# Single float32 products in place of three float32r products, gated sums shared by three engines, and the scores of two units ahead of both value sums

## What is computed

```python
xn = _layernorm(x)
Q = (xn @ Wq.T).reshape(H, b, s, dkh); K = ...; V = ...      # the reshape mixes heads, batches and tokens
scores = einsum('hbqd,hbkd->hbqk', Q, K)
out = einsum('hbqk,hbkd->hbqd', softmax(scores), V).reshape(b, s, -1)
y = out + xn
attention = (y - mean(y, (1, 2))) / sqrt(var(y, (1, 2)) + EPS)
logits = xn @ w_gate.T
top_logits, top_idx = top_k(logits, 2); gates = softmax(top_logits) spread over the 8 experts
ffn = sum over e of gates[:, e] * ((xn @ w_in[e].T) @ w_out[e].T)
return x + attention + ffn
```

## Time and profile before

| what | value |
|---|---|
| median of 3 runs | 1052.1 us (1048.34 to 1052.39) |
| the profiled execution, its own time | 1055.4 us |
| its span, first to last instruction | 1053.6 us |
| PE busy | 1012.4 us (96%) |
| DVE busy | 873.8 us (83%) |
| ACT busy | 627.3 us (60%) |
| POOL busy | 78.7 us (7%) |
| mean granted TensorE clock | 0.981 |
| chain of work that ended last | PE 89%, DVE 5%, DMA 4% |

### The profile page before, as it was taken

One profiled execution on the slowest core, in us unless ns is written; L12 is line 12 of the kernel. 1 busy time (PEld: TensorE's weight loads), 2 busy tenths in 40 slices (PEclk: granted clock), 3 DMA queues, 4 the chain that ended last, 5 costly groups with the idle time before them and its releaser, 6 DMA issues.

```text
span 1053.6 us, 20712 instructions
## 1 busy us (share of the span) xinstructions
PE 1012.4 (96%) x7816; PEld 527.1 (50%) x7816; DVE 873.8 (83%) x1255; ACT 627.3 (60%) x1231; POOL 78.7 (7%) x205
## 2 busy tenths in 40 slices
PE   6778999999999999999999999999999999999995
PEld 6666888888886533333333333333333333333332
DVE  4301777877877989999999999999999999999976
ACT  2100111111110178888888888888888888888885
POOL 2100111011100001000100010001000100010001
PEclk9899999999999989999999999999999999999998
DMA  7777456445555012222222222222222222222214
GB/s 274 271 246 223 130 161 181 129 133 158 144 162 160 5 52 62 71 61 70 62 70 62 69 61 69 62 70 61 70 62 71 60 70 61 71 60 71 63 25 160
DMA packets 127042, 108.58 MB, mean 103 GB/s; under 512 B 81120, under 2 KB 102368, under 8 KB 126944
## 3 DMA queue, kind: packets, MB, share of 16 engines
q1 hardware_dynamic: 114016, 86.03, 29.6%
q10 hardware_dynamic: 12928, 21.24, 5.9%
HBM read 80.75 MB, written 42.21 MB: 117 GB/s over the span
## 4 chain that ended last, share of the span: by engine, by line
PE 89%; DVE 5%; DMA 4%; issue 1%; SPq 0%; ACT 0%; ACTq 0%; POOL 0%; POOLq 0%; DVEq 0%
PE ps L892 27%; PE ps L874 22%; PE ps L829 15%; PE ps L862 11%; PE ps L801 5%; PE ps L775 3%; DMA wp<-w_out_t 3%; PE ps L790 2%; PE ps L903 2%; DVE negm L620 1%; PE ps L915 1%; DVE acc L608 1%; PE ps L763 1%; DVE xnc L733 0%; DMA qf<-ot 0%
## 5 line engine op out<-in xcount | busy, mean ns | idle before, releaser
L620 DVE TENSOR_REDUCE negm<-ps 128x1 f32<-128x1024 f32 x512 | 618.5, 1222 | 31.9 <-PE ps L862 15.3
L464 ACT ACTIVATE wp<-ps 128x512 f32<-128x512 f32 x684 | 369.4, 602 | 88.7 <-PE ps L874 62.6
L874 PE MATMUL ps<-qf,kf 50*128 50x512 f32 x1024 | 388.1, 455 | 2.1 <-DVE ps L679 1.7
L862 PE MATMUL ps<-kf,qf 48*128 48x512 f32 x1024 | 368.1, 451 | 0.2 <-DVE negm L620 0.2
L874 PEld LDWEIGHTS ps<-qf,kf 50*128 50x128 f32 x1024 | 160.5, 186 | 207.4 <-ACT wp L464 107.7
L892 PE MATMUL ps<-wp,vb 128*17 128x256 f32 x2736 | 215.7, 387 | 0.3 <-issue 0.3
L862 PEld LDWEIGHTS ps<-kf,qf 48*128 48x128 f32 x1024 | 146.3, 186 | 7.5 <-issue 5.7
L464 ACT ACTIVATE vstage<-ps 128x512 f32<-128x512 f32 x170 | 102.3, 602 | 24.6 <-PE ps L874 11.2
L829 PE MATMUL ps<-mth,xth 128*128 128x512 f32 x256 | 103.8, 405 | 3.4 <-DVE spare L552 2.4
L892 PEld LDWEIGHTS ps<-wp,vb 128*17 128x17 f32 x2736 | 46.9, 95 | 118.5 <-ACT picks L464 42.8
L464 ACT ACTIVATE picks<-ps 128x512 f32<-128x512 f32 x170 | 102.4, 602 | 0.0
(11 more groups left out here) (104 smaller groups left out, 675.9 us busy)
## 6 DMA issues: line engine op xcount, KB each, us to landing
feat_d<-qk_d SPq DMA_DIRECT2D x64, 256.0 KB, 4.5
qf<-feat_d SPq DMA_DIRECT2D x128, 128.0 KB
wp<-w_in SPq DMA_DIRECT2D x16, 512.0 KB, 4.3
wp<-w_out_t SPq DMA_DIRECT2D x16, 512.0 KB, 5.2
qk_d<-stage ACTq DMA_DIRECT2D x32, 256.0 KB
qk_d<-spare ACTq DMA_DIRECT2D x32, 256.0 KB
qf<-feat_d SPq DMA_DIRECT2D x128, 64.0 KB
kf<-feat_d SPq DMA_DIRECT2D x128, 64.0 KB
```

Source lines behind the costliest of these rows:

```text
L464: nc.scalar.activation(weight_tile(n, j, b)[:, h * HALF:(h + 1) * HALF], ps[:, ST_BANK[(2 * unit + b) % 3], :], ACT.Exp).then_inc(exp_done, 1)
L620: nc.vector.tensor_reduce(negm[:, n % 2, qt:qt + 1], ps[:, b:b + 2, :].rearrange("p b c -> p (b c)"), AX.X, ALU.max, negate=True).then_inc ...
L862: last = nc.tensor.matmul(ps[:, MAX_BANK[turn % 2] + half, :], qf[rows, u, qt * P:(qt + 1) * P], kf[rows, u, :], start=True, stop=True)
L874: nc.tensor.matmul(ps[:, ST_BANK[(2 * unit + half) % 3], :], kf[rows, u, j * P:(j + 1) * P], qf[rows, u, h * HALF:(h + 1) * HALF], start=T ...
```

## The change

- All operands are plain float32; the split halves, their buffers and the instructions that make them are gone (on ACT, DVE and POOL). Each product of three is one float32 product (`project_qk`, `project_v`, `y_bank`).
- In the attention a product has 16 or 17 rows, and the four products of a unit lie on four row groups of 32 rows: the maxima on groups 0 and 1, the scores on groups 2 and 3.
- The gated sums: DVE takes two of the four banks of a tile, ACT scales the other two (`scale_experts`), and POOL adds the pieces (`add_scaled`).
- Six pairs of buffers for expert weights instead of two, and two chunks of tokens projected in the first stage instead of one.
- The stores of Q, K and V are issued by SP instead of ACT; the stored size is halved. A block is regrouped once inside the attention loop, 8 blocks ahead.
- On PE two units' `crossed_scores` stand first (h = 0 and 1), then both `sum_values`.

```diff
-    TERMS = 3
-    FR = DH * TERMS
-    SR = FR + 2
-    ROWS = P // 2
+    GROUP = 32
+    GROUPS = P // GROUP
+    FR = DH
+    SR = FR + 1
...
             def y_bank(t, j):
-                p, tokens = t // TC % 2, slice(t % TC * P, (t % TC + 1) * P)
-                pe.wait_ge(ff_added[j], 2 * t)
-                products = [(v, m, kt) for kt in range(KT) for v, m in ((xth, mth), (xth, mtl), (xtl, mth))]
-                for i, (v, m, kt) in enumerate(products):
-                    last = nc.tensor.matmul(ps[:, Y_BANK[j], :], v[:, p, kt, tokens],
-                                            m[:, kt, 2 * j:2 * j + 2, :].rearrange("p e d -> p (e d)"),
-                                            start=i == 0, stop=i == len(products) - 1)
+                if t and j < BY_VECTOR:
+                    pe.wait_ge(ff_added[j], 2 * t)
+                elif t:
+                    pe.wait_ge(ff_scaled[j - BY_VECTOR], 2 * t)
+                tokens = slice(t % TC * P, (t % TC + 1) * P)
+                for kt in range(KT):
+                    last = nc.tensor.matmul(ps[:, Y_BANK[j], :], xt[:, t // TC % SETS, kt, tokens],
+                                            mt[:, kt, 2 * j:2 * j + 2, :].rearrange("p e d -> p (e d)"),
+                                            start=kt == 0, stop=kt == KT - 1)
...
+            def scale_experts(t, j):
+
+                if j == BY_VECTOR:
+                    if t >= 2:
+                        act.wait_ge(ff_sum, t - 1)
+                    if t % (PAIR * TC) == 0:
+                        act.wait_ge(gates_done, t // (PAIR * TC) + 1)
+                act.wait_ge(y_ready[j], t + 1)
+                for h in range(2):
+                    nc.scalar.activation(scaled_by[:, t % 2, 2 * (j - BY_VECTOR) + h, :], ps[:, Y_BANK[j], h * D:(h + 1) * D],
+                                         ACT.Copy, scale=gates[:, t, 2 * j + h:2 * j + h + 1]
+                                         ).then_inc(ff_scaled[j - BY_VECTOR], 1)
...
+            def add_scaled(t):
+                par, tile = t % 2, acc[:, bass.ds(t, 1), :].rearrange("p o d -> p (o d)")
+                for j in range(E // 2 - BY_VECTOR):
+                    pool.wait_ge(ff_scaled[j], 2 * (t + 1))
+                nc.gpsimd.tensor_tensor(scaled_by[:, par, 0:2], scaled_by[:, par, 0:2], scaled_by[:, par, 2:4], ALU.add
+                                        ).then_inc(ff_step, 1)
...
             def scores(n, j, h, half):
                 u, unit = n % SLOTS, NKT * n + 2 * j + h
                 if j == 0 and h == 0:
                     pe.wait_ge(mrow_in[u], 32 * (n // SLOTS + 1))
                 if unit:
                     pe.wait_ge(exp_done, 2 * unit - 2 + half)
-                rows = half_rows(half, SR)
+                rows = group_rows(GROUPS // 2 + half, SR)
                 nc.tensor.matmul(ps[:, ST_BANK[(2 * unit + half) % 3], :], kf[rows, u, j * P:(j + 1) * P],
                                  qf[rows, u, h * HALF:(h + 1) * HALF], start=True, stop=True
                                  ).then_inc(st_ready[half], 1)
...
                         if n == NB - 2 and j in (1, 3) and h == 0:
                             mean_over_partitions(0, slice(0, EARLY), j // 2)
+                    for h in range(2):
                         if j >= LAG:
                             sum_values(n, j - LAG, h)
                         elif n:
                             sum_values(n - 1, NKT // 2 + j - LAG, h)
-                        if n and j == LAG - 1 and h == 1 and n + 1 < NB:
-                            maxima_to_rows(n + 1)
+                    if n and j == LAG - 1 and n + 1 < NB:
+                        maxima_to_rows(n + 1)
```

More of the change, by code:

```diff
@@ L5 @@
 FP32 = mybir.dt.float32
-FP32R = mybir.dt.float32r
 BF16 = mybir.dt.bfloat16
@@ L223, in feature_loads @@
         def feature_loads(n):
[L225 to L232, removed]
+            for group in range(GROUPS):
+                rows = slice(group * GROUP, group * GROUP + DH)
+                keys = slice(group % 2 * HALF, (group % 2 + 1) * HALF)
+                yield qf, rows, slice(0, POS), feat_d[n, 0]
+                yield kf, rows, slice(0, HALF), feat_d[n, 1, :, keys]
         def value_loads(n, par):
@@ L261, in regroup @@
[L261 to L268, removed]
+                    sp.dma_start(half[slot], w.rearrange("e h d -> (e h) d")[rows, :]
+                                 .rearrange("(p h) d -> p h d", h=HU)).then_inc(w_in_s[slot], 16)
@@ L278, in _ @@
                     load_weights(e, h)
+            for c in range(PAIR):
+                values_out(c)
+                qk_out(c)
             def features(n):
@@ new lines, in second_weight, with qk_copy @@
+            def second_weight(pair):
+                act.wait_ge(gap_done, pair + 1)
+                rows = slice(PAIR * TC * pair, PAIR * TC * (pair + 1))
+                nc.scalar.activation(ex[:, rows], gap[:, rows], ACT.Exp).then_inc(gexp_done, 1)
+            def qk_copy(c, o):
+                if o == 0 and c >= 2:
+                    act.wait_ge(qk_stored[c % 2], 64 * (c // 2))
+                act.wait_ge(project_ready, 2 * TC * c + TC + o + 1)
+                nc.scalar.copy(stage[:, c % 2, o, :], ps[:, PROJECT_BANK[o % 2], :]).then_inc(qk_evac, 1)
@@ new lines, in add_experts @@
+                if j == 0 and t >= 2:
+                    dve.wait_ge(ff_sum, t - 1)
+                dve.wait_ge(y_ready[j], t + 1)
+                for h, total in enumerate((tile, vsum[:, t % 2])):
+                    product = ps[:, Y_BANK[j], h * D:(h + 1) * D]
+                    gate = gates[:, t, 2 * j + h:2 * j + h + 1]
+                    if j:
+                        dve.wait_ge(ff_added[j - 1], 2 * t + h + 1)
+                    if j == 0 and h == 1:
+                        nc.vector.tensor_scalar(total, product, gate, None, ALU.mult).then_inc(ff_added[j], 1)
+                    else:
+                        nc.vector.scalar_tensor_tensor(out=total, in0=product, scalar=gate, in1=total,
+                                                       op0=ALU.mult, op1=ALU.add).then_inc(ff_added[j], 1)
@@ L848, in half_rows @@
-            def half_rows(half, last):
-                return slice(half * ROWS, half * ROWS + last)
+            expert_product(1, 1)
+            for o in range(2, 4):
+                project_qk(0, o)
+            expert_product(2, 0)
+            transposes(1)
+            expert_product(2, 1)
+            for t in range(TC):
+                project_v(1, t)
+            expert_product(3, 0)
+            for o in range(2):
+                project_qk(1, o)
+            expert_product(3, 1)
@@ new lines, in _ @@
+            pe.wait_ge(m_done, KT * E)
+            for t in range(NT - 2 * TC):
+                c, i = t // TC + PAIR, t % TC
+                for j in range(E // 2):
+                    if c < NC:
+                        if i == 0 and j == 0:
+                            transposes(c)
+                        elif i == 1:
+                            project_v(c, j)
+                        elif i >= 2 and j % 2 == 0:
+                            project_qk(c, 2 * (i - 2) + j // 2)
+                    y_bank(t, j)
```

522 lines of the change are left out of this document (238 added, 284 removed).

## The result

The change makes the kernel 1.985 times as long (interval 1.972 to 1.998): a median of 2083.15 us over 4 runs (2082.82 to 2102.67), beside 1052.24 us (1048.34 to 1054.62) for the kernel before. The forecast was 1445 us, with a range of 1365 to 1545. The sign was right, and the size was not: 638 us are missing in it.

The account below looks back on a forecast made before the run. PE was taken to bound the kernel everywhere, level with DVE in the attention. Terms of 400 us before attention, 991 for 256 pairs, 42 per-block and 13.4 tail gave a 1446 us span; forecast 1445 us, range 1365 to 1545.

Parts of the forecast that it names:

- Together 3.87 us a pair: Attention on PE: scores, maxima, the wait for an exponential and two value sums take 3.87 us per two units.
- Before the attention: First and second stage: dearer float32 products, 0.86 us at 512 columns, make attention start at 400 instead of 361.8 us.
- Four row groups side by side: Attention on PE: a unit's four score and maxima products run at once, 0.97 us with the late start.
- two at a time: Rival for the attention: the four row groups don't all run side by side; 4.62 us a pair, 1637 in all; 6%.
- program order: Rival for the attention: each float32 product's second record holds back the next product; 5.05 us a pair, 1747 in all; 3%.
- estimate of 4.13: Attention: with four row tiles at 3.07 times one, a unit's products take 1.12 us, a pair 4.13, some 1510 in all.
- The wait: Attention on PE: the second unit's fourth score product waits for an exponential to free its bank, 0.86 us a pair.
- The rival in which it is covered: Rival for the attention: the fourth score product needn't wait; a pair is 2.90 us, 1197 in all; 6%.
- a pair without the wait: Attention in the new order, fourth score product not waiting: 0.11 + 1.72 + 0.08 + 0.99 = 2.90 us.
- What is covered: ACT, DVE and POOL work hides under PE before the attention, ACT and DVE in it; DVE busy 61% of attention.
- 0.65 us a block: Attention, per block: transposes 0.21 + 0.29 and 0.15 for the sums' copy on ACT; 42 us over 64 blocks.
- The tail: After the attention: 15.4 us after the last scores, 2 of it already in the pair, so 13.4 us.

Follow-up runs that it names:

- experiment 2: The kernel after with scores and maxima products addressing all 32 rows of each group, added rows zero in one operand: 1427.43 us.
- experiment 9: The kernel before with five pairs of weight buffers instead of two and 64 rows instead of 50 in the score products: 1037.32 us, 0.9854 times before.
- experiment 6: The kernel before with only the high halves in its attention, so products on 16 and 18 rows instead of 48 and 50: 1511.49 us against 1054.97.
- experiment 5: The kernel after with 32 rows in scores and maxima, and each unit's value sums put back behind its own scores: 1318.57 us.
- experiment 7: The kernel after with 32 rows in the score products alone, the maxima's products staying at 16 rows: 1443.32 us.
- experiment 1: The kernel after with each unit's value sums put back behind its own scores, the pairing alone undone: 2002.05 us.

## Why the prediction was wrong, and where it was right

**The step that failed.** The forecast for a pair of units, "Together 3.87 us a pair", is a sum of durations that were all read at full clock, and the total took all 256 pairs at it: "256 pairs x 3.87 = 991". No term and no rival asked what clock the changed products would be granted. The earlier trace rows shows 0.99 for the attention, but for products on 48 and 50 rows; those of the change are on 16 and 17. The runs put 6.59 us a pair in its place. By experiment 2 that is 2083 - 1427 = 656 us, all of the miss and a little more: with the clock kept, the change comes out at 1427 us, 18 below the forecast and within its own range of 1405 to 1485.

**What was there to be seen.** The kernel before has a stretch that should have raised the question, and I didn't split its attention far enough to see it: from 364.0 to 377.6 us its PE is busy all but without a gap and gets 0.50 (the stretches under experiment 9). The mean of 0.99 over 676.4 us hid it. It isn't shown to be the same thing in small: it is on 48 and 50 rows, behind 1.71 us of idle time. From 326.4 to 329.8 us, 0.5 us behind an idle time of 2.44 us, the same kernel has a clock of 0.51 even for products nearly all on 128 rows. But a stretch where the clock is low though PE is busy would have named a rival: half clock for all of the attention. With the pair as measured since, that is 400 + 256 x 6.59 and some 40, over 2100 us.

The Trainium skill, "TensorE: Matmul & The Clock Gate", section "What's actually happening", has the clock that TensorE is granted set by how busy PE has been recently, with two levels only. The trace agrees on the two levels and not on the cause, if busy is read as the profile counts it: PE was busy 1300.33 of 1300.50 us at a mean of 0.52. Here the measurement decides, and experiments 2 and 6 say what moves it over a whole attention: the rows that the products address, with PE equally busy.

**Before the attention: right.** Single float32 products are dearer than three float32r ones by what was worked out. In the kernel after the records of gated and Q, K products start 0.43 us apart:

```profile
199.86 1.88 PE L763 MATMUL ps<-xt,wqk 128*128 128x512 f32 x4
201.58 1.88 PE L832 MATMUL ps<-mt,xt 128*128 128x512 f32 x4
```

(201.58 - 199.86) / 4 = 0.43, so 0.86 a product of 512 columns. The second stage began at 90 us as forecast, and the attention at 397.7 for 400. These products are on all 128 rows, at a clock of 1.00.

**Four row groups side by side: right.** "L832 and L763 records 0.43 us apart" and "four score and maxima products starting within some 0.02 us" both came. PE's timeline at the start of a pair at full clock:

```profile
740.50 0.69 PE L876 MATMUL ps<-qf,kf 17*128 17x512 f32 x1
740.50 0.70 PE L864 MATMUL ps<-kf,qf 16*128 16x512 f32 x2
740.52 1.10 PE L876 MATMUL ps<-qf,kf 17*128 17x512 f32 x2
```

A score record and two maxima records start at 740.50, and the fourth group's at 740.52. So neither "two at a time" (4.62 us a pair) nor "program order" (5.05) is what happens. The prediction named a rule of the Trainium skill ("TensorE: Matmul & The Clock Gate", section "Part 3: Packing small matmuls — row/col tiling"), that products start and end strictly in program order. The starts here don't agree with it: the first records of all four products start before the second record of the first. Nor does the pair agree with the estimate of 4.13 us by that section's packing figure: it is 3.84.

**The wait: right in place, size and cause.** It was forecast at 0.86 us for a pair, released by an exponential, and stands at 746.15 - 745.31 = 0.84. The rival in which it is covered (1197 us) falls with it. At half clock the two loads are as far apart, 0.88 us, but a record takes twice as long there, so that the neighbours' second records fill most of it. Against the other order it costs less, 0.43 us a pair (experiment 5): there a unit takes 1.68 us in the chain (804.56 to 806.24), a pair 3.36, where my own figure for a pair without the wait was 2.90. That figure was for the new order; the old one turns the array twice as often, which by my own terms is 0.11 + 0.08 = 0.19 us more. What fills the rest of the 0.46 wasn't taken apart.

**What is covered: right.** ACT, DVE and POOL bounded nothing before the attention but for waits of a microsecond or so, and in the attention DVE and POOL bounded nothing, and ACT only by the wait above. DVE was to be busy for 61% of the attention; at full clock it is 630.35 of 1014.30 us, 62% (experiment 2).

**Per block and tail.** I had 0.65 us a block. In experiment 2, 1014.3 us of attention less 256 x 3.85 leaves 28.7 us, 0.45 a block, 13 us less in all. The tail was 14.1 us for 13.4. With 2.7 us before the attention and 5 from the pair, that is what the forecast's sum (1446) has over this span (1425.7).

**Where the 1031 us came from**, in spans: 2081.2 - 1425.7 = 655.5 by the clock; 397.3 - 361.8 = 35.5 before the attention; 1014.3 - 676.4 = 337.9 in the attention at full clock, for float32's second record and the wait; and 1.3 back in the tail. Together 1027.6, the difference of the spans.

**What stays open.** Why the clock came back for three stretches of some 31 us with the same work under way wasn't found out, nor why it was lost at the end of experiment 7, nor what the dips at the start of the attention come from. It wasn't tried whether added rows in the maxima alone would do, or what the value sums' few columns do to the clock.

## What to carry to other kernels

Ask of each change what it does to the share of the array that the products address, before taking a duration from the old trace: a duration is worth only what its clock is worth, and here the clock was worth 656 us of 1031. Where a busy TensorE shows half the clock, address the free rows too, with zeros in one operand: the products took no more time for it here (a pair is 3.85 us against 3.84), and the clock may come back. And a merge of several products into one can be dearer in time if it needs a slower type: three float32r products of 512 columns cost 0.69 us, the one float32 product in their place 0.86.

## What the runs showed of the hardware that was not expected

- The granted clock was 0.50 over 1136.6 us with PE busy for all of them (experiment 6), and 0.50 over 1587.2 us (experiment 1).
- Rows that hold only zeros in one operand kept the clock up as rows do in use: 1.00 over 1014.3 us with 32 rows, of which 15 or 16 add nothing (experiment 2).
- At half clock a pair isn't twice as long: 6.59 against 3.84 us. The load that waits for the exponential starts 0.88 us after its neighbour's, against 0.84, since the exponential doesn't follow TensorE's clock. Without a wait it comes near: the value sums of a pair take 1.84 against 0.99.
- The same products on the same rows ran at 1.00 in one kernel and at 0.50 in another (the end of experiments 2 and 7, from 1390.2 us), with PE busy in both.
- Four float32 products on four row groups start side by side at both clocks (within 0.02 us, at 740.50 and at 1204.59 us in the kernel after), so a float32 product's second record doesn't hold back the next product on another group.
